# Projection of a transformer layer: weight loads, their low parts, rope sums and low parts of N on other engines

## The chip, the cores and the metric

The kernel runs on one core of one Trainium2 chip. The metric is the time of one execution on the device, in microseconds (us). The engines are TensorE (PE in the profile), VectorE (DVE), ScalarE (ACT), GpSimd (POOL) and SyncE (SP), which issues transfers; each has a queue of its own, worked off in order, and they meet only at semaphores.

## The reference

A macaron layer on x of 2048 tokens by 512: half a mixture of experts, attention, half a mixture of experts.

```python
x = x + 0.5 * _L0_ffn_ref(_layernorm(x), router_w, w1, w2, w3)      # 8 experts, top 2
x = x + _L0_attn_ref(_layernorm(x), wq, wk, wv, wo)
x = x + 0.5 * _L0_ffn_ref(_layernorm(x), router_w, w1, w2, w3)

# in _L0_attn_ref: 16 heads of 32 for q, 4 for k and v, causal
q = (x @ wq).reshape(b, t, QH, HD).transpose(0, 2, 1, 3)
k = (x @ wk).reshape(b, t, KVH, HD).transpose(0, 2, 1, 3)
v = (x @ wv).reshape(b, t, KVH, HD).transpose(0, 2, 1, 3)
q = apply_rope(q, cos, sin)      # x * c + rotate_half(x) * s
k = apply_rope(k, cos, sin)
```

All is fp32. The stage that this change touches is the layer norm before attention, the products with wq, wk, wv, and the rope.

## The kernel before

The program has stages, one after the other on every engine: a first norm and router, the experts (39 blocks of 128 rows, whose results are scattered to a tensor `y` in device memory, two halves of 2048 rows), the projection, attention, a second router, the experts again. The projection is written in `sp_project`, `pool_project`, `dve_project`, `act_project` and `pe_project`.

**Tiles.** The projection works on 16 tiles of 128 tokens. For tile i the input is three parts, x rows and the two halves of y, summed into `p.X[:, i % 4]` (four buffers, `XA` in the trace). For tiles 0 to 3, SP loads the halves into `ST` and VectorE adds them (L1150). For tiles 4 to 15, SP loads the x rows and GpSimd issues two adding transfers of y, one after the other (L1132): the first waits for the x rows, the second for the first.

**Precision.** A fp32 matrix product is made for tiles 1 to 13 from three passes of fp32r operands: high part times high part, high times low, low times high. `WQ` is the weights in fp32, `WH` (`WQH`) their high part, a cast by ScalarE, and `WL` (`WQL`) the difference WQ - WH. Tiles 0, 14 and 15 use one fp32 pass on `WQ`. The rotated q and k are stacked in `N` (`NA`): ScalarE writes the rounded high part twice (L1249, L1251, semaphore `ndup`) and the difference, the low part, is written beside it (L1196, L1197, semaphore `pN`).

**One turn i** of each engine, in the order of its queue:
- VectorE: row maxima of tops (`dve_top`, L965 and L967), found maxima, `norm(i+2)` (statistics), then `rope_split(i)`: two products of rope (L1182 to L1184, semaphore `rope`), their sum `t1 += t2` (L1186, `rsum`), `low(i+1)` (L1171), `scale(i+2)` (L1165), the low parts of N (L1196, L1197). `rope_split(i)` begins by waiting for `pN` of tile i-1, since `t1` is used again.
- ScalarE: the turned tile as high part, the square root for tile i+2, five copies of the stacked tile i-1 to `Qs` and `Ks` (L1239), V (L1244), the high parts of N, and, where maxima are found, `mT` (L1004).
- TensorE: projection i, transposes of tile i+1, stack of tile i-1 (20 transposes, L1330). Between the products of projections from tile 5 on it computes 6 tops (L952), scores of attention's first groups of which VectorE takes the maxima; they share three PSUM banks with the stack.
- SP: x rows of tile i, the rope table of tile i (`turns(i)`, waits for rope(i-3)), and the found maxima of tile i-3 (`sp_found`): a store of `mT` to device memory, a wait for it, a load into `Qs`. So the x rows of tile i+4 are issued behind rope(i), and behind `sp_found` where tile i has one. Maxima are found in turns 7, 10, 12 and 15.
- GpSimd: for tile i+4 the two adding transfers; four memsets of `Ks` rows (L1135), one behind each of rows 6 to 9.

**The start.** All engines wait until the last scatters of the experts have landed (`all_written`). SP then issues the rows of tile 0, the three weight loads, and the rows of tiles 1 to 3. ScalarE casts the weights after root(0), turned(0) and root(1); GpSimd computes `WL`.

**Memory.** `WQ` lies at the start of the area `A_T`, `XA` behind it; the area is shared with buffers of the experts.

Of the kernel before, what the change touches and what calls it, by code (L numbers as in the profile page):

```python
# [11 lines left out]
NJ = 39  # L12
# [197 lines left out]
def memory(nc, ctx, g):  # L210
    ctx.enter_context(nc.sbuf_tensor("fence", [P, (END - BASE) // 4 - 8], F32))
    keep = Area(nc, KEEP, END)
    g.Kc = keep("K", [P, C_PAD + 2])
    g.KB = keep("KB", [P, CBW], BF16)
    g.RT = keep("RT", [P, 4 * HD])
    g.PM = keep("PM", [P, 2, 16, 4])
    g.NM = keep("NM", [P, 16])
    g.M2 = keep("M2", [P, 4, 2, 4], F32R)
    g.mT = nc.alloc_sbuf_tensor_at("mT", [8, BQ], F32R, offset=keep.at)
    g.SM = keep("SM", [P, BQ])  # L220
    g.ones = keep("ones", [P, HD])
    g.ident = g.Kc[:, C_ID:C_ID + P]

    low = Area(nc, Q0, Q2)
    g.X = low("X0", [P, NT, D])
    g.R0 = router_memory(0, low, Area(nc, E_BIG, KEEP), 2)
    g.W = [weight_memory(nc, 0, Q0, Q2, A_K), weight_memory(nc, 1, Q3, Q1, Q0)]
    g.r = [route_memory(nc, f) for f in range(2)]
    g.x = [expert_memory(nc, f) for f in range(2)]

    g.Qs = [nc.alloc_sbuf_tensor_at(f"Qs{b}", [P, QH, BQ], F32R, offset=Q0 + 32 * KB1 * b) for b in range(NB)]
    g.Ks = nc.alloc_sbuf_tensor_at("Ks", [P, KVH, T], F32R, offset=A_K)
    g.V = nc.alloc_sbuf_tensor_at("V", [P, NT, P], F32, offset=A_V)
# [848 lines left out]

def sp_project(g):
    s, sp, d, p = g.s, g.nc.sync, g.d, g.p
    all_written(g, sp.wait_ge)

    x = d["L0_attn_x"].rearrange("b t d -> (b t) d")

    def rows(i):
        if i >= 4:  # L1090
            sp.wait_ge(s("paT"), i - 3)
        sp.dma_start(p.X[:, i % 4, :], x[i * P:i * P + P, :]).then_inc(s(f"xa{i % 4}"), 16)
        if i < 4:
            for h in range(2):
                sp.dma_start(p.ST[:, 2 * i + h, :], g.yd[T * h + i * P:T * h + i * P + P, :]).then_inc(s(f"st{i}"), 16)

    def turns(i):
        if i >= 3:
            sp.wait_ge(s("rope"), i - 2)
        sp.dma_start(p.cs[:, i % 3, :], d["rope"][i * P:i * P + P, :]).then_inc(s(f"cs{i % 3}"), 16)  # L1100

    rows(0)
    for name, o, n in (("wq", 0, 512), ("wk", 512, 128), ("wv", 640, 128)):
        sp.dma_start(p.WQ[:, :, o:o + n], d[f"L0_attn_{name}"].rearrange("(k p) n -> p k n", p=P)).then_inc(s("wqkv"), 16)
    turns(0)
    for i in range(1, 4):
        rows(i)
    for i in range(1, NT + 4):
        if 4 <= i < NT:
            rows(i)  # L1110
        if i < NT:
            turns(i)
        for G in g.found.get(i - 3, ()):
            sp_found(g, G)


def pool_project(g):
    s, pool, p = g.s, g.nc.gpsimd, g.p
    all_written(g, pool.wait_ge)

    pool.memset(g.ones[:], 1.0).then_inc(s("ones"), 1)
    for j, (o, n) in enumerate(((0, 512), (512, 256))):
        pool.wait_ge(s("wqh"), j + 1)
        pool.tensor_tensor(p.WL[:, :, o:o + n], p.WQ[:, :, o:o + n], p.WH[:, :, o:o + n].bitcast(F32),
                           ALU.subtract).then_inc(s("wql"), 1)
    for i in range(4, NT):
        b = i % 4
        pool.wait_ge(s(f"xa{b}"), 16 * (i // 4 + 1))
        for h in range(2):
            if h:  # L1130
                pool.wait_ge(*halves_on(g, i, 1))
            pool.dma_start(p.X[:, b, :], g.yd[T * h + i * P:T * h + i * P + P, :], accum_op=ALU.add).then_inc(  # L1132
                halves_on(g, i, h + 1)[0], 16)
        if 6 <= i < 6 + KVH:
            pool.memset(g.Ks[96:98, i - 6, :].bitcast(F32), 1.0).then_inc(s("kone"), 1)  # L1135


def dve_project(g):
# [34 lines left out]
    def rope_split(i):  # L1173
# [8 lines left out]
        dve.tensor_tensor(hd(p.t1[:]), qk, p.cs[:, b, 0:32].unsqueeze(1).to_broadcast([P, 20, HD]), ALU.mult)  # L1182
        dve.tensor_tensor(hd(p.t2[:])[:, :, 0:16], qk[:, :, 16:32], turn(32), ALU.mult)
        dve.tensor_tensor(hd(p.t2[:])[:, :, 16:32], qk[:, :, 0:16], turn(48), ALU.mult).then_inc(s("rope"), 1)  # L1184
        dve.wait_ge(s("rope"), i + 1)
        dve.tensor_tensor(p.t1[:], p.t1[:], p.t2[:], ALU.add).then_inc(s("rsum"), 1)  # L1186
        if in_parts(i + 1):
            low(i + 1)
        r = hd(p.t1[:])
        if i + 2 < NT:  # L1190
            scale(i + 2)
        dve.wait_ge(s("rsum"), i + 1)
        dve.wait_ge(s("ndup"), i + 1)
        if i:
            dve.wait_ge(*turned_from_n(g, i - 1))
        dve.tensor_tensor(p.N[:, 0:16, 64:96], r[:, 0:16, :], Nf[:, 0:16, 0:32], ALU.subtract)  # L1196
        dve.tensor_tensor(p.N[:, 16:20, 32:64], r[:, 16:20, :], Nf[:, 16:20, 0:32], ALU.subtract).then_inc(s("pN"), 1)  # L1197

    norm(0)
    scale(0)  # L1200
    norm(1)
    scale(1)
    for i in range(NT + 1):
        for _, key in g.fill[i]:
            dve_top(g, key)
        for G in g.found[i]:
            dve_found(g, G)
        if i + 2 < NT:
            norm(i + 2)
        if i < NT:  # L1210
            rope_split(i)


def act_project(g):
# [26 lines left out]
    def doubled(i):  # L1241
# [5 lines left out]
        if i:  # L1247
# [3 lines left out]
        act.copy(p.N[:, 16:20, :].rearrange("p h (a d) -> p h a d", d=HD)[:, :, 0:3:2, :],  # L1251
                 r[:, 16:20, :].unsqueeze(2).to_broadcast([P, 4, 2, HD])).then_inc(s("ndup"), 1)

    root(0)
    turned(0)
    root(1)
    act.wait_ge(s("wqkv"), 48)
    for o, n in ((0, 512), (512, 256)):
        act.copy(p.WH[:, :, o:o + n], p.WQ[:, :, o:o + n]).then_inc(s("wqh"), 1)
    for i in range(NT + 1):  # L1260
        if i + 1 < NT:
            turned(i + 1)
# [669 lines left out]
```

## Time and profile before

| | |
|---|---|
| runs | 1379.84, 1383.33, 1377.25 us |
| median | 1379.84 us |
| profiled execution | 1382.4 us, its span 1381.1 us |
| TensorE busy in the span | 1221.9 us, 88% |
| VectorE | 884.9 us, 64% |
| ScalarE | 661.7 us, 48% |
| GpSimd | 551.0 us, 40% |
| granted TensorE clock, mean | 0.958 of full speed |

The span is from the first to the last instruction of one execution. A busy share over the whole span is a mean over stages with different limits, so a stage is read by windows, by the timeline and by the chain of waits, each limited to it. Line numbers (L1184) are those of the kernel before. In the timeline a name such as `XA<-y` says what is written from what; in square brackets stand the idle time of the engine just before, and what ended it.

### The profile page before, as it was taken

How to read it: one execution, taken by the hardware profiler on the slowest of the kernel's cores; microseconds unless marked ns; L12 is line 12 of the kernel's file. 1: busy time of each engine (PE TensorE's matmuls, PEld its weight loads, DVE VectorE, ACT ScalarE, POOL GpSimd, SP SyncE). 2: the span in 40 equal slices, each digit the busy share in tenths (PEclk: the TensorE clock that was granted, in tenths of full speed). 3: DMA queues.
4: the chain of work that ended last, by engine and by line, in shares of the span. 5: the costliest groups of instructions: out<-in, count | busy, mean ns of one | idle time of the engine just before them, and what ended most of it. 6: DMA issues, size and time to landing. Idle time of an engine off the chain costs nothing.

```text
span 1381.1 us, 22056 instructions
## 1 busy us (share of the span) xinstructions
PE 1221.9 (88%) x7484; PEld 784.2 (57%) x7484; DVE 884.9 (64%) x2056; ACT 661.7 (48%) x1313; POOL 551.0 (40%) x458
## 2 busy tenths in 40 slices
PE   4499999679888999999989999999999849988884
PEld 4478888557775554454445455454433347766663
DVE  7867777479996665666676675667620375655662
ACT  2545555335455543454355454465567524444441
POOL 5635444223110110013344454527458653444443
PEclk8689999889999999999999999999999969999998
DMA  9723333355540021042013003023000343555554
GB/s 333 312 92 107 107 109 110 110 136 96 89 67 32 2 63 32 32 93 32 32 62 63 2 1 124 1 93 62 2 1 1 133 184 84 91 90 93 90 89 61
DMA packets 56891, 114.42 MB, mean 83 GB/s; under 512 B 7664, under 2 KB 17136, under 8 KB 56752
## 3 DMA queue, kind: packets, MB, share of 16 engines
q0 software_dynamic: 26112, 68.17, 22.5%
q1 hardware_dynamic: 30672, 44.85, 9.6%
q8 instruction: 64, 1.05, 0.3%
q14 instruction: 43, 0.35, 0.1%
HBM read 79.71 MB, written 33.55 MB: 82 GB/s over the span
## 4 chain that ended last, share of the span: by engine, by line
PE 57%; DMA 19%; DVE 14%; issue 5%; ACT 4%; SPq 1%; POOL 0%; POOLq 0%; DVEq 0%; ACTq 0%
DMA out<-Y,DI 13%; PE bank L1493 10%; PE bank L1505 10%; PE bank L797 8%; PE bank L952 8%; PE bank L1518 5%; PE bank L820 4%; PE bank L1555 3%; DVE PM L965 3%; DMA XA<-y 2%; DVE bank L967 2%; PE bank L779 1%; ACT P L1597 1%; PE bank L1535 1%; PE bank L1313 1%
## 5 line engine op out<-in xcount | busy, mean ns | idle before, releaser
L1597 ACT ACTIVATE P<-bank 128x512 f32<-128x512 f32 (+3 forms) x640 | 305.6, 536 | 299.6 <-PE bank L1493 295.5
L965 DVE TENSOR_REDUCE PM<-bank 128x1 f32<-128x512 f32 x384 | 252.8, 685 | 100.6 <-PE bank L952 99.6
L1493 PE MATMUL bank<-Qs,Ks 98*128 98x512 f32 (+3 forms) x640 | 248.5, 413 | 8.0 <-ACT P L1597 6.3
L952 PE MATMUL bank<-Ks,Qs 96*128 96x512 f32 (+3 forms) x640 | 238.9, 392 | 8.8 <-DVE PM L965 5.3
L1493 PEld LDWEIGHTS bank<-Qs,Ks 98*128 98x128 f32 x640 | 117.6, 190 | 151.3 <-issue 86.0
L1651 POOL TENSOR_TENSOR CH<-CH,P 128x512 f32<-128x512 f32 x128 | 160.3, 1286 | 71.9 <-ACT P L1597 71.0
L1636 POOL TENSOR_SCALAR_AFFINE_SELECT P<-P 128x512 f32<-128x512 f32 x64 | 40.9, 638 | 308.5 <-ACT P L1597 308.5
L967 DVE CUSTOM_DVE_ANT_0 bank<-bank,KB 128x128 f32<-128x128 f32 (+3 forms) x256 | 124.7, 497 | 57.8 <-PE bank L952 57.0
L952 PEld LDWEIGHTS bank<-Ks,Qs 96*128 96x128 f32 x640 | 121.9, 191 | 63.0 <-DVE PM L965 32.2
L1505 PE MATMUL bank<-P,V 128*32 128x512 f32 (+3 forms) x1280 | 152.5, 548 | 0.2 <-POOL P L1636 0.2
L908 DVE TENSOR_TENSOR DL<-W,DH 128x512 fp32r<-128x512 f32 x152 | 98.4, 689 | 46.4 <-ACT DH L869 33.7
L762 POOL DMA_INDIRECT out<-Y,DI x39 | 64.6, 1657 | 124.7 <-DMA out<-Y,DI 98.7
L735 POOL DMA_INDIRECT XG<-xn,TK x78 | 94.0, 1205 | 50.5 <-issue 21.9
L869 ACT CAST DH<-W 128x512 fp32r x152 | 86.8, 618 | 25.4 <-issue 25.4
L1518 PE MATMUL bank<-P,ones 128*32 128x512 f32 (+3 forms) x896 | 96.7, 503 | 0.0
L797 PE MATMUL bank<-WH,XH 128*128 x312 | 94.0, 423 | 3.0 <-ACT XH L849 2.0
L797 PE MATMUL bank<-WL,XH 128*128 x312 | 87.3, 402 | 0.1
L797 PE MATMUL bank<-WH,XL 128*128 x312 | 87.0, 401 | 0.0
L890 DVE TENSOR_TENSOR XL<-bank,XH 128x512 fp32r<-128x512 f32 x78 | 53.9, 691 | 46.3 <-ACT XH L849 46.3
L849 ACT CAST XH<-bank 128x512 fp32r<-128x512 f32 x78 | 45.8, 587 | 67.8 <-PE bank L779 64.9
L759 POOL DMA_INDIRECT y<-Y,DI x39 | 38.3, 983 | 98.2 <-DVE Y L916 98.2
L779 PE MATMUL bank<-K,XG 128*128 128x128 f32 x312 | 49.4, 282 | 28.6 <-DMA XG<-xn,TK 28.6
(184 smaller groups left out, 1903.3 us busy)
## 6 DMA issues: line engine op xcount, KB each, us to landing
xn<-XN SPq DMA_DIRECT2D x8, 1024.0 KB, 6.7
WR<-L_ffn_w POOLq DMA_DIRECT2D x16, 512.0 KB, 15.5
XO<-y POOLq DMA_DIRECT2D x8, 1024.0 KB, 9.6
WR<-L_ffn_w SPq DMA_DIRECT2D x16, 512.0 KB, 7.6
XA<-y POOLq DMA_DIRECT2D x24, 256.0 KB, 4.2
W<-L_ffn_w POOLq DMA_DIRECT2D x8, 512.0 KB, 25.0
XA<-L_attn_x SPq DMA_DIRECT2D x16, 256.0 KB, 3.4
XO<-L_attn_x SPq DMA_DIRECT2D x4, 1024.0 KB, 7.9
```

What stands on the lines that cost most here:

```text
L735: pool.indirect_dma_start(out=x.XG[:, j % NG, :], out_offset=None, in_=g.xnd[f][:, :], in_offset=bass.IndirectOffsetOnAxis(ap=r.TK[:, j:j ...
L797: ins = pe.matmul(bk(g, 2 + j % 2), part[:, k * P:k * P + P], w[:, bass.ds(ev[j] * 2048 + k * 512, 512)], start=(n == 0 and k == 0), stop= ...
L869: act.copy(x.DH[:, k, :], W.W3[:, bass.ds(e * 1024 + k * 512, 512)]).then_inc(s("dh"), 1)
L908: ins = dve.tensor_tensor(x.DL[:, k, :], W.W3[:, bass.ds(e * 1024 + k * 512, 512)], DHf[:, k, :], ALU.subtract)
L952: pe.matmul(bk(g, bank)[:, 0:n], g.Qs[b][0:96, G % 4 * 4 + h, c * P:c * P + P], g.Ks[0:96, G % 4, k * BQ:k * BQ + n], start=True, stop=Tru ...
L965: dve.tensor_reduce(dst, bk(g, bank)[:, 0:n], AX.X, ALU.max).then_inc(s(f"free{bank}"), 1)
L967: dve.tensor_tensor_reduce(out=bk(g, bank)[:, 0:n], in0=bk(g, bank)[:, 0:n], in1=g.KB[:, CB_MASK + BQ - n:CB_MASK + BQ], scale=1.0, scalar ...
L1493: pe.matmul(bk(g, i % 3)[:, o:BQ], g.Ks[0:98, G % 4, k * P:k * P + P], g.Qs[G // 4][0:98, G % 4 * 4 + j, o:BQ], start=True, stop=True).the ...
L1505: ins = pe.matmul(bk(g, 3)[32 * h:32 * h + 32, o:BQ], g.V[:, k, q * HD:q * HD + HD], a.P4[buffer_of(n)][:, h, o:BQ], start=(k == 0), stop= ...
L1518: ins = pe.matmul(bk(g, 4)[32 * h:32 * h + 32, o:BQ], g.ones[:], a.P4[buffer_of(n)][:, h, o:BQ], start=fresh, stop=last)
L1597: act.activation(a.P4[buffer_of(n)][:, j, o:BQ], bk(g, i % 3)[:, o:BQ], ACT.Exp, scale=scale).then_inc(s("exp"), 1)
L1651: ins = pool.tensor_tensor(to[:, h, :], two[:, h, :], one[:, h, :], ALU.add)
```

## The change

- SP issues the three loads of `WQ` at the head of `sp_project`, when TensorE's last expert product is done (`yp`), ahead of the wait for the scatters. For that `XA` and `WQ` change places in memory: `WQ` then overlaps only expert buffers that are read by then, and `XA` lies where GpSimd's scatter offsets were.
- ScalarE casts the weights first, before root(0).
- `WL` is computed by VectorE, after scale(1), instead of by GpSimd.
- The rope sum and the low parts of N go from VectorE to GpSimd. GpSimd's loop now runs over the turns i = 0 to 15: wait rope(i), sum; first adding transfer of tile i+4; memset where i is 6 to 9, and a wait for it; low parts of N; second adding transfer of tile i+4.

```diff
     t = Area(nc, A_T, KEEP)
+    p.X = t("XA", [P, 4, D])
     p.WQ = t("WQ", [P, 4, 768])
-    p.X = t("XA", [P, 4, D])
...
 def sp_project(g):
+    sp.wait_ge(s("yp"), NJ)
+    for name, o, n in (("wq", 0, 512), ("wk", 512, 128), ("wv", 640, 128)):
+        sp.dma_start(p.WQ[:, :, o:o + n], d[f"L0_attn_{name}"].rearrange("(k p) n -> p k n", p=P)).then_inc(s("wqkv"), 16)
     all_written(g, sp.wait_ge)
...
     rows(0)
-    for name, o, n in (("wq", 0, 512), ("wk", 512, 128), ("wv", 640, 128)):
-        sp.dma_start(p.WQ[:, :, o:o + n], d[f"L0_attn_{name}"].rearrange("(k p) n -> p k n", p=P)).then_inc(s("wqkv"), 16)
     turns(0)
...
 def pool_project(g):
-    for j, (o, n) in enumerate(((0, 512), (512, 256))):
-        pool.wait_ge(s("wqh"), j + 1)
-        pool.tensor_tensor(p.WL[:, :, o:o + n], p.WQ[:, :, o:o + n], p.WH[:, :, o:o + n].bitcast(F32),
-                           ALU.subtract).then_inc(s("wql"), 1)
-    for i in range(4, NT):
-        b = i % 4
-        pool.wait_ge(s(f"xa{b}"), 16 * (i // 4 + 1))
-        for h in range(2):
-            if h:
-                pool.wait_ge(*halves_on(g, i, 1))
-            pool.dma_start(p.X[:, b, :], g.yd[T * h + i * P:T * h + i * P + P, :], accum_op=ALU.add).then_inc(
-                halves_on(g, i, h + 1)[0], 16)
+    def half_on(i, h):
+        if h:
+            pool.wait_ge(*halves_on(g, i, 1))
+        else:
+            pool.wait_ge(s(f"xa{i % 4}"), 16 * (i // 4 + 1))
+        pool.dma_start(p.X[:, i % 4, :], g.yd[T * h + i * P:T * h + i * P + P, :], accum_op=ALU.add).then_inc(
+            halves_on(g, i, h + 1)[0], 16)
+
+    for i in range(NT):
+        pool.wait_ge(s("rope"), i + 1)
+        pool.tensor_tensor(p.t1[:], p.t1[:], p.t2[:], ALU.add).then_inc(s("rsum"), 1)
+        if i + 4 < NT:
+            half_on(i + 4, 0)
+        pool.wait_ge(s("rsum"), i + 1)
         if 6 <= i < 6 + KVH:
             pool.memset(g.Ks[96:98, i - 6, :].bitcast(F32), 1.0).then_inc(s("kone"), 1)
+            pool.wait_ge(s("kone"), i - 5)
+        pool.wait_ge(s("ndup"), i + 1)
+        if i:
+            pool.wait_ge(*turned_from_n(g, i - 1))
+        pool.tensor_tensor(p.N[:, 0:16, 64:96], r[:, 0:16, :], Nf[:, 0:16, 0:32], ALU.subtract)
+        pool.tensor_tensor(p.N[:, 16:20, 32:64], r[:, 16:20, :], Nf[:, 16:20, 0:32], ALU.subtract).then_inc(s("pN"), 1)
+        if i + 4 < NT:
+            half_on(i + 4, 1)
...
 def dve_project(g):
-        dve.wait_ge(s("rope"), i + 1)
-        dve.tensor_tensor(p.t1[:], p.t1[:], p.t2[:], ALU.add).then_inc(s("rsum"), 1)
         if in_parts(i + 1):
             low(i + 1)
-        r = hd(p.t1[:])
         if i + 2 < NT:
             scale(i + 2)
-        dve.wait_ge(s("rsum"), i + 1)
-        dve.wait_ge(s("ndup"), i + 1)
-        if i:
-            dve.wait_ge(*turned_from_n(g, i - 1))
-        dve.tensor_tensor(p.N[:, 0:16, 64:96], r[:, 0:16, :], Nf[:, 0:16, 0:32], ALU.subtract)
-        dve.tensor_tensor(p.N[:, 16:20, 32:64], r[:, 16:20, :], Nf[:, 16:20, 0:32], ALU.subtract).then_inc(s("pN"), 1)
+
+    def weights():
+        for j, (o, n) in enumerate(((0, 512), (512, 256))):
+            dve.wait_ge(s("wqh"), j + 1)
+            dve.tensor_tensor(p.WL[:, :, o:o + n], p.WQ[:, :, o:o + n], p.WH[:, :, o:o + n].bitcast(F32),
+                              ALU.subtract).then_inc(s("wql"), 1)
...
     scale(1)
+    weights()
...
 def act_project(g):
+    act.wait_ge(s("wqkv"), 48)
+    for o, n in ((0, 512), (512, 256)):
+        act.copy(p.WH[:, :, o:o + n], p.WQ[:, :, o:o + n]).then_inc(s("wqh"), 1)
     root(0)
     turned(0)
     root(1)
-    act.wait_ge(s("wqkv"), 48)
-    for o, n in ((0, 512), (512, 256)):
-        act.copy(p.WH[:, :, o:o + n], p.WQ[:, :, o:o + n]).then_inc(s("wqh"), 1)
```

## Rows read from the trace of the kernel before

**Rows 1.** The windows between turns: from:to, length, busy time of each engine, clock, DMA

```profile
265.59:295.35 29.76, 10.81 (x33) 6.54 (x34) 16.39 (x29) 4.52 (x7) 8.51 (x4) 0.71 0.52 180
295.35:325.93 30.58, 27.99 (x183) 24.36 (x183) 26.29 (x62) 17.56 (x39) 7.96 (x8) 0.95 0.55 100
325.93:353.75 27.82, 24.86 (x164) 21.00 (x163) 27.02 (x85) 13.82 (x32) 9.58 (x9) 1.00 0.53 89
353.75:373.23 19.48, 16.89 (x114) 14.42 (x113) 17.71 (x54) 9.66 (x23) 3.51 (x5) 1.00 0.54 87
383.07:403.44 20.37, 16.91 (x114) 14.43 (x113) 18.35 (x58) 9.66 (x23) 3.95 (x5) 1.00 0.46 83
403.44:429.62 26.18, 25.68 (x147) 19.56 (x145) 22.39 (x67) 13.57 (x30) 0.34 (x1) 1.00 0.10 14
```

**Rows 2.** The chain that ended last, start of the stage: start us, us, what

```profile
287.74 4.94 DVE XA L1150
```

**Rows 3.** Timeline (start us, us, engine, line, operation) and landing of one weight load

```profile
281.17 7.21 PE L1313 MATMUL bank<-WQ,SM 128*128 128x512 f32 x16 [0.68 <-ACT SM L1228]
287.45 7.43 POOL L1124 TENSOR_TENSOR WQL<-WQ,WQH 128x2048 fp32r<-128x2048 f32 x2 [17.84 <-ACT WQH L1259]
...
WQ<-L_attn_wv SPq DMA_DIRECT2D x1, 256.0 KB, 8.8
```

**Rows 4.** Timeline of VectorE in turns 4 and 7

```profile
328.25 1.11 DVE L1165 TENSOR_SCALAR XA<-XA,mvA,smA 128x512 f32<-128x512 f32 x1
...
352.13 0.83 DVE L1182 TENSOR_TENSOR t<-bank,cs 128x640 f32<-128x640 f32 x1
...
353.79 0.83 DVE L1186 TENSOR_TENSOR t<-t,t 128x640 f32<-128x640 f32 x1
...
356.53 0.68 DVE L1196 TENSOR_TENSOR NA<-t,NA 128x512 fp32r<-128x512 f32 x1
357.13 0.28 DVE L1197 TENSOR_TENSOR NA<-t,NA 128x128 fp32r<-128x128 f32 x1
```

**Rows 5.** Timeline of TensorE and VectorE, the tops; in brackets idle time and releaser

```profile
330.48 0.50 PE L952 MATMUL bank<-Ks,Qs 96*128 96x512 f32 x1 [0.55 <-DVE PM L967]
...
409.42 0.43 DVE L967 CUSTOM_DVE_ANT_0 bank<-bank,KB 128x256 f32<-128x256 f32 x1 [0.17 <-PE bank L952]
```

**Rows 6.** Timeline of GpSimd, first additions in turns 4, 6, 7, 9, 10

```profile
329.33 0.85 POOL L1132 DMA_DIRECT2D XA<-y  x1 [0.26 <-DMA XA<-L_attn_x]
...
349.44 0.85 POOL L1132 DMA_DIRECT2D XA<-y  x1 [3.00 <-DMA XA<-L_attn_x]
...
361.85 0.85 POOL L1132 DMA_DIRECT2D XA<-y  x1 [7.03 <-DMA XA<-L_attn_x]
...
379.24 0.85 POOL L1132 DMA_DIRECT2D XA<-y  x1 [5.25 <-issue]
...
391.85 0.85 POOL L1132 DMA_DIRECT2D XA<-y  x1 [7.31 <-DMA XA<-L_attn_x]
```

**Rows 7.** Timeline of SP's queue, the x rows of tile 11

```profile
358.95 0.36 SPq L1092 DMA_DIRECT2D XA<-L_attn_x  x1
```

**Rows 8.** Instructions of one line: count, duration ns min/median/max, first and last start

```profile
L553 POOL TENSOR_TENSOR WL<-WR,WH x4: 4523/4536/4562, 36.6 to 50.0; 128x2048 fp32r<-128x2048 f32 x4
L553 DVE TENSOR_TENSOR WL<-WR,WH x1: 2286/2286/2286, 59.9 to 59.9; 128x2048 fp32r<-128x2048 f32 x1
...
L1135 POOL MEMSET Ks<- x4: 1802/1806/1815, 319.9 to 344.6; 2x2048 f32 x4
...
L1651 POOL TENSOR_TENSOR CH<-CH,P x128: 1252/1278/1473, 650.2 to 1071.2; 128x512 f32<-128x512 f32 x128
```

**Rows 9.** Windows as in rows 1, about two gaps of TensorE

```profile
267.00:268.00 1.00, 0.00 (x0) 0.00 (x0) 0.00 (x0) 0.00 (x0) 0.60 (x1) 0.86 0.00 0
...
1258.00:1260.00 2.00, 2.00 (x8) 1.71 (x7) 0.54 (x1) 0.59 (x1) 0.22 (x1) 0.50 0.79 146
```

**Rows 10.** Timeline of VectorE, low parts of the last tile

```profile
432.00 0.69 DVE L1196 TENSOR_TENSOR NA<-t,NA 128x512 fp32r<-128x512 f32 x1 [1.51 <-ACT NA L1251]
```

More of the change, by code:

```diff
@@ L1121, in pool_project @@
     pool.memset(g.ones[:], 1.0).then_inc(s("ones"), 1)
-    for j, (o, n) in enumerate(((0, 512), (512, 256))):
-        pool.wait_ge(s("wqh"), j + 1)
-        pool.tensor_tensor(p.WL[:, :, o:o + n], p.WQ[:, :, o:o + n], p.WH[:, :, o:o + n].bitcast(F32),
-                           ALU.subtract).then_inc(s("wql"), 1)
-    for i in range(4, NT):
-        b = i % 4
-        pool.wait_ge(s(f"xa{b}"), 16 * (i // 4 + 1))
-        for h in range(2):
-            if h:
-                pool.wait_ge(*halves_on(g, i, 1))
-            pool.dma_start(p.X[:, b, :], g.yd[T * h + i * P:T * h + i * P + P, :], accum_op=ALU.add).then_inc(
-                halves_on(g, i, h + 1)[0], 16)
+    hd = lambda ap: ap.rearrange("p (h d) -> p h d", d=HD)
+    Nf = p.N[:].bitcast(F32)
+    r = hd(p.t1[:])
+    def half_on(i, h):
[11 more added lines that the diff above has]
+        pool.wait_ge(s("rsum"), i + 1)
         if 6 <= i < 6 + KVH:
             pool.memset(g.Ks[96:98, i - 6, :].bitcast(F32), 1.0).then_inc(s("kone"), 1)
+            pool.wait_ge(s("kone"), i - 5)
[6 more added lines that the diff above has]
+            half_on(i + 4, 1)
 def dve_project(g):
```

## The prediction

> **What bounds the kernel now.** The page puts 88% of the span on TensorE, but that is an average; the change touches one stage, so I read the windows whose borders are the rope turns of the projection [rows 1]. I call tile i's turn complete at R(i), the end of the second half of `t2` on VectorE (L1184), a little over 1.6 us after its beginning: R(0) = 295.35, R(4) = 325.93, R(7) = 353.75, R(9) = 373.23, R(10) = 383.07, R(12) = 403.44, R(15) = 429.62 us, and attention starts at 436.63. The windows show four regimes. Up to R(0) TensorE works 10.8 of 29.8 us: the stage waits for data. From R(0) to R(4), four turns in 30.58 us, VectorE has 4.3 us spare. From R(4) to R(7), three turns in 27.82 us, VectorE is busy 27.02 us: it is the bound, 9.3 us a turn. From R(12) on TensorE is (25.68 of 26.18 us). Outside 265.59 to 436.63 us nothing is changed.
>
> The chain of waits of the start [rows 2] runs through one addition on VectorE that takes 4.94 us; its twin just before took about 0.7. Beside it [rows 3] GpSimd computes the low weights from 287.45 to 294.88: the addition ends with GpSimd's first piece.
>
> **Part 1, the start.** New order: the three weight loads are issued at about 265.6, when TensorE's last expert matmul is done, instead of 270.8 to 272.3; ScalarE casts them first; VectorE makes the low parts after scale(1); GpSimd's 7.43 us there are gone. R(0) worked out: rows of tile 0 are issued as before, after the scatters have landed, so norm(0) starts at about 274.9 and scale(0) ends at 279.2 as before. Tile 1's halves no longer queue behind 1.5 MB of weights, so norm(1) and scale(1), 4.2 us together, run directly behind: end 283.5. Low weights on VectorE: 3072 elements at the rate of the 2048 in 2.29 us [rows 8], 3.4 us, end 286.9. norm(2), 2.5 us without the blocked addition, ends 289.4; TensorE's first projection ends at 288.4 [rows 3], so it isn't later. The rope multiplications take 1.62: R(0) = 291.1, a gain of 4.25 us. Bounds: the last weight load took 8.8 us to land [rows 3]; at that price the cast ends at 278.7 and sits in front of root(0), 1.2 us of the gain gone. Above, 5.5 us if tile 0 isn't delayed and VectorE is the only limit.
>
> The trace shows the blocking as whole waits, not a slowdown. By the Trainium skill (SBUF — State Buffer, Who interferes with whom) a VectorE instruction with two SBUF inputs contends with a GpSimd instruction that reads SBUF, and one of them blocks for a whole instruction; the 4.94 us addition agrees. By that rule the same lock returns with each rope sum on GpSimd, against `scale`; that is a rival below.
>
> **Part 2, what leaves VectorE in each turn.** The rope sum (0.83 us busy) and the two low parts of N (0.68 and 0.28) [rows 4]; by the starts of what followed them they are 0.74 + 0.80 = 1.54 us a turn. The rope multiplications before them take 1.62, from 352.13 to R(7). This is worth 1.54 us only if nothing is right behind. TensorE is: between R(4) and R(5) it waited for VectorE only 0.55 us, and between R(12) and R(13) VectorE already waited for TensorE's sixth and last top [rows 5], which it took at R(12)+6.0; with 0.35 for it, 1.05 for the statistics and 1.62 for the rope that turn lasted 9.0 us, VectorE idle in it. The sixth top is 256 or 512 columns wide in turn, so TensorE's loop gives 8.8 to 9.2. VectorE's 9.3 can fall to that, 0.1 to 0.5 us a turn, not by 1.5.
>
> **Part 3, the order on GpSimd.** This is the step on which I stake the forecast. GpSimd's queue for turn i is now: wait rope(i), sum; wait for the landing of x rows i+4, issue the first addition of y; memset (i = 6 to 9); wait `ndup`, low parts of N; wait for the first addition to land, issue the second. VectorE's rope(i+1) waits `pN` from the low parts. So the low parts, which need only R and the copies of ScalarE, stand behind the landing of x rows, which SP issues only after rope(i) and, in turns 7 and 10, after the round trip of the maxima. Terms:
> - GpSimd's rates [rows 8]: 2048 elements 4.54 us, 512 elements 1.28 us, so 2.12 ns an element and 0.19 fixed. Sum of 640: 1.55. Low parts 512 + 128: 1.28 + 0.46 = 1.74. An issue 0.85, the memset 1.81, both seen.
> - When the first issue for tile i+4 came, after R(i) [rows 6]: 3.4 (turn 4), 4.9 (turn 6), 8.1 (turn 7), 6.0 (turn 9), 8.8 (turn 10). In turn 7 the round trip holds back the x rows to 358.95, R+5.2 [rows 7]; it begins after ScalarE's copies, which now follow GpSimd's slower sum, +0.65.
> - Turn length by this loop = that moment + 0.9 issue + (1.9 memset) + 1.74 + 0.1 + 1.62 rope = moment + 4.4, or + 6.3 with memset.
>
> Turn by turn against before: turns 0 to 3 have moments of 3.4 to 4.0, so 7.8 to 8.4 against 7.5 to 7.9: +1.8 in all. Turns 4 and 5 are held by TensorE's loop: -0.2. Turns 6, 8 and 9: the longer turns leave the transfers more room, so I take 4.4 between the seen 3.4 and 6.0: 10.7 each against 9.24, 10.04 and 9.84, +3.0. Turn 7: 8.1 + 0.65 + 6.3 = 15.05 against 9.44, +5.6. Turn 10: 8.8 + 0.65 + 4.4 = 13.8 against 8.99, +4.8. Turn 11 before was 11.4 because x was late, and now x is early: about 10.5, -0.9. Turns 12 to 14 issue nothing for a later tile and TensorE bounds them: 0. Tail: between R(15) and attention the low parts are on the path, begun at 432.00 after ScalarE's copies [rows 10]; the sum (1.55 for 0.83, of which ScalarE hid some) and the low parts (1.74 for 0.8) give +1.8.
>
> TensorE now idles about 6 us in turn 7 and 4 in turn 10. After TensorE's last expert matmul at 265.6 its granted clock averaged 0.86 in the window 267 to 268, and a shorter gap near 1256 was followed by a window at 0.50, which is 1.2 GHz of 2.4, with TensorE busy in all of it [rows 9]. I estimate 1.7 us of work lost per such restart, from about 3.4 us at that level; it falls beside GpSimd's waiting in turn 8 and I have put it into turn 11's 10.5.
>
> Sum: -4.25 + 1.8 - 0.2 + 3.0 + 5.6 + 4.8 - 0.9 + 1.8 = +11.65, say +12 us. The profiled execution has a span of 1381.1 us in 1382.4; it becomes about 1393 in 1394.5. The median of the runs shown is 1379.84, so I forecast 1392.
>
> Unknown costs, from both sides. The low parts of N are written in pieces of 32 elements, which no GpSimd row shows: not under the 1.74 us of contiguous rows; above, I take up to 2.6 (half as much again), 0.9 us in some nine turns, +8. The moments of turns 6, 8, 9 at 3.4: -3; as seen (4.9, 5.2, 6.0): +2.9. The clock: 0 to +3. The start: -1.2 to +1.2. Together 1384 to 1402 for this case.
>
> **The rivals.**
> - A, faster: x rows are landed early enough and the stage stays VectorE's. From the turn's budget (rope to rope 9.3, rope itself 1.6) the low parts may end as late as R+5.9 to 7 without cost; with a moment of 3.4 they end at R+6.0. For it: turns 0 and 4 with moments of 3.4. Against it: the two round trips, which no spare VectorE time shortens, and TensorE's loop. If the full 1.54 us came in turns 4 to 11: -4.25 - 12.3 + 1.8 = -14.8, 1365 us. It decides if pN comes before R+6.1 in nearly every turn. 12 in 100 for anything below 1373.
> - B, a wash: the start gives 4.25, only the two round trips cost, and their delay is partly given back since VectorE catches up: -4.25 - 1 + 7 + 1.8 = +3.5, 1383 us. For it: turn 11's slack. 20 in 100.
> - C, GpSimd's pieces of 32 cost double, 3.5 us: +1.75 in ten turns above the forecast, 1409 us. Nothing in the trace speaks for it but the absence of a row. 7 in 100.
> - D, the lock of part 1 comes back: `scale` (which took 1.11 us in turn 4 beside GpSimd's memset [rows 4]) waits for each rope sum. GpSimd may start a sum 1 us late, behind its issue, so scale ends up to 1.1 us later, and the tops with it; where VectorE has no slack that is 8 x 1.1 = +9 over the forecast, 1401 us. The skill's rule above is the same mechanism. 6 in 100.
> - E, the start gains nothing, as the early weights only delay tile 0's rows: forecast + 4.25, 1396 us; 5 in 100.
>
> **How the numbers follow.** The forecast has 50 in 100. A measurement of this kernel can tell about 0.5%, 6.9 us, from no change. Slower by more (above 1386.7): the forecast, C, D and E, 68 in 100. Within: B, 20. Faster: A, 12. The range reaches from just under B to the upper bounds: 1380 to 1402.
>
> **What would show it.** Right: the low weights gone from GpSimd, R(0) near 291; in turns 7 and 10 rope(i+1) starts 13 and 12 us after R(i), waiting for GpSimd's low parts, behind an issue that waited for XA; memset between issue and low parts in turns 6 to 9; TensorE idle for `NA` there, with half clock after. Wrong: rope(i+1) nowhere waits for pN, or turns 4 to 9 are near 8 us (A); the low parts last 2.5 us or more (C); scale stretched in every turn with VectorE full (D).

## The result, and the profile after

The changed kernel took 1400.88 us (median of 4 runs, 1398.0 to 1405.95) against 1379.8 (median of 4 runs, 1377.25 to 1383.33): ratio 1.0155, 95% interval 1.0117 to 1.0193. (The ratio is that of the means.) It is slower, as forecast, by 21 us where 12 were forecast. The profiled execution took 1398.0 us, its span 1396.8, granted clock 0.958 on average, as before.

The page of the changed kernel, its span and busy times:

```profile
span 1396.8 us, 22056 instructions
PE 1223.9 (88%) x7484; PEld 787.0 (56%) x7484; DVE 865.9 (62%) x2010; ACT 665.2 (48%) x1313; POOL 596.6 (43%) x504
```

VectorE lost 19 us of work and GpSimd gained 46; TensorE's share did not move. The page says who works, not who waits, so the reading is again by windows. These answer to [rows 1]: the start, turns 0 to 3, then turns 6, 7, 8, 9 and 10 one by one (turn i goes from R(i) to R(i+1); in the changed kernel R(i) is the end of L1199), turns 12 to 14, and the tail from R(15) to attention. The columns are from:to, length, busy time of TensorE, of its weight loads, of VectorE, ScalarE and GpSimd, granted clock, busy share of the DMA engines and GB/s.

```profile
263.60:293.06 29.46, 10.46 (x26) 5.74 (x27) 15.46 (x32) 4.52 (x7) 1.08 (x2) 0.65 0.55 182
293.06:326.10 33.04, 27.25 (x187) 23.80 (x185) 22.24 (x52) 17.83 (x38) 19.37 (x19) 1.00 0.53 93
344.10:354.47 10.37, 7.99 (x54) 7.05 (x53) 8.81 (x29) 4.84 (x11) 7.67 (x7) 0.97 0.47 83
354.47:369.78 15.31, 10.18 (x55) 8.76 (x54) 7.83 (x25) 5.03 (x11) 6.72 (x6) 0.83 0.31 55
369.78:381.89 12.11, 9.31 (x61) 8.41 (x60) 7.35 (x26) 5.41 (x12) 6.69 (x6) 0.92 0.41 71
381.89:393.89 12.00, 10.37 (x62) 8.95 (x61) 8.79 (x28) 5.33 (x13) 6.66 (x6) 0.89 0.48 72
393.89:406.98 13.09, 8.13 (x49) 7.00 (x48) 7.34 (x25) 4.42 (x10) 4.10 (x4) 0.93 0.31 61
418.49:444.73 26.24, 25.75 (x147) 19.61 (x145) 18.34 (x59) 13.95 (x30) 9.69 (x9) 1.00 0.04 8
444.73:454.58 9.85, 4.62 (x27) 3.88 (x25) 0.00 (x1) 7.18 (x13) 3.20 (x3) 0.83 0.02 5
```

Turn 7 shows the new state: in 15.31 us TensorE works 10.2, VectorE 7.8, ScalarE 5.0, GpSimd 6.7. No engine is the bound; they wait for each other. In turns 12 to 14, where nothing is fetched for a later tile, the time is that of before (26.24 against 26.18). Turn 7 on the timeline, GpSimd, SP, TensorE and VectorE in order of time:

```profile
354.55 1.53 POOL L1137 TENSOR_TENSOR t<-t,t 128x640 f32<-128x640 f32 x1 [0.99 <-DVE t L1199]
...
360.56 0.36 SPq L1095 DMA_DIRECT2D XA<-L_attn_x  x1
...
363.58 0.85 POOL L1132 DMA_DIRECT2D XA<-y  x1 [7.49 <-DMA XA<-L_attn_x]
364.48 1.80 POOL L1142 MEMSET Ks<- 2x2048 f32 x1
366.36 1.26 POOL L1147 TENSOR_TENSOR NA<-t,NA 128x512 fp32r<-128x512 f32 x1
367.58 0.45 POOL L1148 TENSOR_TENSOR NA<-t,NA 128x128 fp32r<-128x128 f32 x1
...
368.09 3.76 PE L1343 MATMUL bank<-K,NA 128*96 128x128 f32 x20 [5.13 <-POOL NA L1148]
368.17 0.82 DVE L1197 TENSOR_TENSOR t<-bank,cs 128x640 f32<-128x640 f32 x1 [3.90 <-POOL NA L1148]
```

GpSimd's sum is done 1.6 us after R(7). Then the queue stands for 7.49 us at the wait for the x rows, which SP issued at 360.56; issue, memset and low parts follow one after the other, and both TensorE's stack and VectorE's next rope start when the second low part ends, 368.0. The waits of the stage from 293 to 455 us (who waited for what: total us, times, longest):

```profile
POOL XA L1132 <- DMA XA<-L_attn_x: 29.5, 9, 7.5
...
PE bank L1343 <- POOL NA L1148: 28.4, 12, 5.1
...
DVE t L1197 <- POOL NA L1148: 14.0, 9, 4.0
```

Where the time went, in the two profiled executions (before, after; us):

| part of the stage | before | after | difference | forecast |
|---|---|---|---|---|
| last expert product of TensorE to R(0) | 29.77 | 29.46 | -0.3 | -4.25 |
| turns 0 to 3 | 30.58 | 33.04 | +2.5 | +1.8 |
| turns 4, 5 | 18.58 | 18.00 | -0.6 | -0.2 |
| turns 6, 8, 9 | 29.12 | 34.48 | +5.4 | +3.0 |
| turn 7 | 9.44 | 15.31 | +5.9 | +5.6 |
| turn 10 | 8.99 | 13.09 | +4.1 | +4.8 |
| turn 11 | 11.38 | 11.51 | +0.1 | -0.9 |
| turns 12 to 14 | 26.18 | 26.24 | +0.1 | 0 |
| R(15) to attention | 7.01 | 9.85 | +2.8 | +1.8 |
| sum | 171.05 | 190.98 | +19.9 | +11.65 |

The spans differ by 15.7: outside the stage this one execution of after was 4.2 us shorter (2.0 before it, 2.2 behind it). The experiments show such differences in both directions, so I read the stage against itself and leave them.

### The profile page after: what moved, and what is told of

Read it like the earlier page. It is cut to its first block, busy times and chain, and to the rows that moved or that the text cites. A ratio compares the mean times of both kernels' runs of the same rounds, so it can differ in the third digit from the quotient of the medians.

```text
span 1396.8 us, 22056 instructions
## 1 busy us (share of the span) xinstructions
PE 1223.9 (88%) x7484; PEld 787.0 (56%) x7484; DVE 865.9 (62%) x2010; ACT 665.2 (48%) x1313; POOL 596.6 (43%) x504
## 4 chain that ended last, share of the span: by engine, by line
PE 63%; DMA 14%; DVE 12%; issue 5%; POOL 3%; ACT 3%; SPq 0%; POOLq 0%; DVEq 0%; ACTq 0%
PE bank L797 10%; PE bank L1506 10%; PE bank L1518 9%; DMA out<-Y,DI 9%; PE bank L952 8%; PE bank L1531 5%; PE bank L820 5%; PE bank L1568 3%; DVE PM L965 3%; PE bank L1326 2%; PE bank L779 2%; DMA XA<-y 1%; PE bank L1343 1%; ACT P L1610 1%; DVE bank L967 1%
## 5 line engine op out<-in xcount | busy, mean ns | idle before, releaser
L1343 PE MATMUL bank<-K,NA 128*96 128x128 f32 x320 | 46.2, 306 | 30.6 <-POOL NA L1148 28.4
## 6 DMA issues: line engine op xcount, KB each, us to landing
WR<-L_ffn_w POOLq DMA_DIRECT2D x16, 512.0 KB, 15.7
```

## The experiments

Two kinds of number follow. The stage's parts come from one profiled execution of each kernel; the medians and ratios from several runs beside the kernel before on the same chip. The medians of before there were 1380.15 us (e1 to e4), 1381.05 (e5 to e8) and 1378.87 (e9 to e11). The ratios are those on record for each kernel; they aren't the quotients of these medians (for e2 and e3 the quotients are higher, 1.012 and 1.016). The tail ends with TensorE's first attention matmul.

| kernel | median us | ratio (95%) | start to R(0) | R(0) to R(15) | tail |
|---|---|---|---|---|---|
| before | 1379.8 | | 29.77 | 134.27 | 7.01 |
| after | 1400.88 | 1.0155 (1.0117 to 1.0193) | 29.46 | 151.67 | 9.85 |
| e1 start only | 1377.91 | 0.9973 (0.9949 to 0.9998) | 29.49 | 135.13 | 7.00 |
| e2 turns only | 1396.86 | 1.0091 (1.0060 to 1.0123) | 28.43 | 154.52 | 9.67 |
| e3 low parts ahead | 1401.71 | 1.0120 (1.0077 to 1.0164) | 29.41 | 155.52 | 10.34 |
| e4 memsets early | 1394.79 | 1.0092 (1.0066 to 1.0117) | 28.63 | 145.84 | 9.93 |
| e5 after, no additions | 1374.42 | 0.9959 (0.9936 to 0.9982) | 29.13 | 126.60 | 9.43 |
| e6 before, no additions | 1376.25 | 0.9950 (0.9919 to 0.9981) | 29.75 | 128.90 | 7.02 |
| e7 start in order | 1374.74 | 0.9965 (0.9944 to 0.9986) | 25.20 | 132.71 | 8.06 |
| e8 low parts shared | 1371.27 | 0.9919 (0.9887 to 0.9951) | 24.77 | 129.80 | 7.76 |
| e9 after, x rows first | 1387.90 | 1.0072 (1.0049 to 1.0096) | 29.14 | 142.93 | 10.49 |
| e10 after, sums back | 1402.07 | 1.0172 (1.0133 to 1.0212) | 29.34 | 151.73 | 9.64 |
| e11 e7, x rows first | 1370.36 | 0.9944 (0.9925 to 0.9964) | 26.36 | 132.47 | 8.41 |

**Each part alone.** My theory: the start gains, and GpSimd's order costs in the turns. Rival: the start gains nothing (E). e1 takes the first half of the change (memory, loads, casts, low weights on VectorE), e2 the second.

```diff
  e1: before, and
+ sp: the three loads of WQ behind yp, ahead of all_written
+ act: casts of WQ ahead of root(0);   dve: WL in weights() behind scale(1)
- pool: WL
  e2: before, and pool_project and the end of each turn of dve_project as in the change
```

> The start of the change alone (weight loads at the end of the experts, casts first, low weights by VectorE after scale(1)); rope sums and low parts of N stay on VectorE, GpSimd issues only the additions and memsets. Theory 'the loads delay the scatters': in the changed kernel the last scatters landed 7.6 us after their issue where they took 2.7 before, so the rows of tile 0 start 5 us late and the gain of the start is spent: from TensorE's last expert matmul to R(0) 29.5 us against 29.77 before, stage and time unchanged within 1 us. Rival, my prediction's part 1: R(0) 4.25 us earlier, time about 1375.5 us (-0.3%).

> The other half alone: loads, casts and low weights as before, rope sums and low parts of N on GpSimd in the order of the change. Theory 'all of the loss is in the turns': R(0) to R(15) 151 to 152 us against 134.3 before, tail 9.8 against 7.0, the whole stage +20 us, time +1.4 to +1.5%. Rival 'start and turns make each other worse' (rows of tiles 0 to 3 come differently): less than +15 us here.

e1: start 29.49 us, so the early loads gave nothing. The ratio of 0.9973 is 0.3% below before, which the stage (171.62 us against 171.05) doesn't account for. e2: turns 154.5 us, 20 more than before and 2.5 above what I expected, with turns 7 and 10 at 15.5 and 14.0; the ratio of 1.0091 lies under the 1.4 to 1.5% expected. The loss is in the turns and the tail, not in the start. Why the start fails is seen in when GpSimd goes on after the last scatters of the experts (issue, then the first instruction behind the landing). e1:

```profile
267.65 0.96 POOL L759 DMA_INDIRECT y<-Y,DI  x1 [1.53 <-DVE Y L916]
274.94 0.12 POOL L1122 MEMSET ones<- 128x32 f32 x1 [6.34 <-DMA y<-Y,DI]
```

The kernel before:

```profile
266.64 0.96 POOL L759 DMA_INDIRECT y<-Y,DI  x1 [1.52 <-DVE Y L916]
269.49 0.12 POOL L1121 MEMSET ones<- 128x32 f32 x1 [1.89 <-DMA y<-Y,DI]
```

The last scatter is waited for until 7.3 us after its issue where it was 2.9, with 1.5 MB of weights in the transfers beside it; every engine waits for it (`all_written`), and counted from TensorE's last expert product tile 0's rows start 4.4 us later. The thirteen traces divide without exception: the seven kernels with early loads wait 7.0 to 7.6 us, the six others 2.8 or 2.9.

**The start in another order.** If that is the cause, the weights must be kept behind the scatters and behind the rows of tiles 0 and 1, and VectorE's part of the gain must come back.

```diff
  e7: before, and
     rows(0)
+    rows(1)
     (loads of WQ as before; casts as before)
+ dve: WL in weights() behind scale(1);   - pool: WL
```

> The kernel before with the weight loads behind the rows of tiles 0 and 1 (and, as before, behind the scatters), casts where they were, and low weights by VectorE behind scale(1). Theory 'the early loads spent the gain by delaying the scatters': here the scatters land in 2.7 us and VectorE is not blocked by GpSimd, so from TensorE's last expert matmul to R(0) 25.6 us against 29.8; stage and time -4 us, ratio 0.997. Rival 'the start is bound by the bytes to load whatever their order': R(0) within 1 us of before.

GpSimd in e7, at the same place:

```profile
265.72 0.96 POOL L759 DMA_INDIRECT y<-Y,DI  x1 [1.52 <-DVE Y L916]
268.56 0.12 POOL L1122 MEMSET ones<- 128x32 f32 x1 [1.88 <-DMA y<-Y,DI]
```

The start is 25.20 us, 4.6 less than before, and the scatter lands as it did. The gain that I worked out for the start exists; the early loads were what took it away. Its size moves between traces: e8 and e11 have the same start and took 24.77 and 26.36 us. In e11 TensorE's first projection waited 2.30 us for the last weight load, in e7 0.94. e7 makes two edits at once, and no run parts them; nor does any run move the loads alone, without the casts and the low weights.

**The low parts ahead of the addition.** If the low parts suffer only from standing behind the x rows, putting them first should win most of the loss.

```diff
  e3: after, in pool_project
-        if i + 4 < NT:
-            half_on(i + 4, 0)
...
         pool.tensor_tensor(p.N[:, 16:20, 32:64], ...).then_inc(s("pN"), 1)
+        if i + 4 < NT:
+            half_on(i + 4, 0)
         (memset behind this, then half_on(i + 4, 1))
```

> The changed kernel with the low parts of N ahead of the first addition and of the memset in GpSimd's queue; the same work on the same engines. Theory 'order': the low parts end at about R+5.0 in every turn, turns 7 and 10 fall from 15.3 and 13.1 to 9 or 10 us, the clock stays high there; the first addition moves back from R+3.4 to 4.9 to at least R+5.0, which makes the early turns 8.3. Stage +5 us over before instead of +20, time +0.3 to +0.4% against before. Rival 'place': the cost is GpSimd's slower sum and low parts and the restarts of the clock, not the order; then at least +14 us remain.

I was wrong: 155.5 us in the turns, no better than after, and the stage 24 us over before, which the rival 'place' had asked for (at least +14); e5 and e6 below decide between the two. GpSimd in turn 5 of e3, and the sum of turn 6:

```profile
346.07 1.27 POOL L1142 TENSOR_TENSOR NA<-t,NA 128x512 fp32r<-128x512 f32 x1 [1.52 <-issue]
347.29 0.46 POOL L1143 TENSOR_TENSOR NA<-t,NA 128x128 fp32r<-128x128 f32 x1
347.69 0.84 POOL L1132 DMA_DIRECT2D XA<-y  x1
352.26 0.86 POOL L1132 DMA_DIRECT2D XA<-y  x1 [3.73 <-DMA XA<-y]
352.85 1.88 POOL L1137 TENSOR_TENSOR t<-t,t 128x640 f32<-128x640 f32 x1
```

The low parts now start 1.5 us after the sum, but the wait for the first addition's landing, 3.73 us and formerly hidden in part under memset and low parts, now stands in front of the next rope sum, which starts 3.4 us after R(6) = 349.50. Sum 1.9, copies of ScalarE 1.5, low parts 1.7, first addition issued and waited for 4.6: about 10 us a turn, above the 9.3 of before (turns 1 to 6 took 9.7 to 10.2). The queue has two waits for transfers in each turn; moving the work round them changes which work pays.

The long turns hardly shrank either: turn 7 took 14.59 us and turn 10 13.56, where I had expected 9 or 10. In turn 7 the low parts were done at R(7)+8.6, but the next rope started only at R(7)+13.0, and not for want of them. ScalarE and TensorE in turn 7 of e3:

```profile
365.08 1.04 ACT L1263 CAST NA<-t 128x1024 fp32r<-128x1024 f32 x1 [3.74 <-POOL t L1137]
...
366.34 0.57 ACT L1004 CAST mT<-bank 8x512 fp32r<-8x512 f32 x1
...
366.96 0.33 PE L952 MATMUL bank<-Ks,Qs 96*128 96x128 f32 x1 [2.92 <-ACT mT L1004]
```

ScalarE's queue holds the copy `mT` behind the high parts of N, and these wait 3.74 us for GpSimd's late sum. TensorE's next top waits 2.92 us for `mT`, the remaining tops and VectorE's maxima follow, and the x rows of tile 11 are issued at R(7)+9.0. So a late sum on GpSimd has a second way to reach VectorE, through ScalarE and TensorE, in the turns in which maxima are found.

**The waits taken away.** e5 and e6 leave out the two additions of y for tiles 4 to 15, so for these tiles y isn't added; the work on the engines is otherwise the same.

```diff
  e5: after, and e6: before, with
-            half_on(i + 4, 0) / (i + 4, 1)        (e6: the dma_start of both halves)
...
-            dve.wait_ge(*halves_on(g, i, 2))
+            dve.wait_ge(s(f"xa{b}"), 16 * (i // 4 + 1))
```

> The changed kernel without the adding transfers of y for tiles 4 to 15 (those tiles are projected from the x rows alone, a part of the residual sum is left out): GpSimd's queue then holds only sums, memsets and low parts, the same work on the same engines, with no wait for a landing among it. Theory 'GpSimd is one serial queue, and waits for landings stand in it between work that VectorE's next turn awaits': turns 7 and 10 fall to 9.5 or less, the clock stays high, turns 4 to 11 are 8.9 to 9.2 each as TensorE allows; R(0) to R(15) 128 to 131 us instead of 151.7. Rival 'place': GpSimd's slower sum and low parts cost by themselves, R(0) to R(15) stays above 140.

> The kernel before with the same adding transfers left out, as the measure for the run above. VectorE holds turns 4 to 11 at 9.3 (no late rows: turns 8 and 11 lose their 0.7 and 2.0 us), turns 0 to 3 shrink to about 6.5 to 7; R(0) to R(15) about 128. Against it the changed kernel without additions should be between -3 and +3 us over R(0) to R(15) by the theory, and +12 or more by the rival.

GpSimd in turn 7 of e5, from R(7) = 348.90 on:

```profile
348.98 1.56 POOL L1137 TENSOR_TENSOR t<-t,t 128x640 f32<-128x640 f32 x1 [3.52 <-DVE t L1195]
350.60 2.05 POOL L1140 MEMSET Ks<- 2x2048 f32 x1
352.73 1.29 POOL L1145 TENSOR_TENSOR NA<-t,NA 128x512 fp32r<-128x512 f32 x1
```

With no landing to wait for, the moved work costs nothing: 126.6 us in the turns against 128.9 with the work on VectorE. With the landings the same move costs 17.4 (151.67 against 134.27). So 17 us of loss and 2 us of gain are told apart: the additions in GpSimd's queue are the loss, and the rival 'place' falls for the turns. e5 takes away their issues (0.85 us each) together with their waits; of the two, e4 and e9 below show what shorter or earlier waits give back, and no run takes away the issues alone. Only the tail stays longer, by 2.4 (9.43 against 7.02): the low parts of the last tile end 1.5 us later on GpSimd, whatever the transfers do, and the stack behind them took 3.59 us for 2.56, the clock again (last section).

**Which waits.** e4 moves the four memsets of GpSimd ahead of the loop, e9 lets SP issue the x rows of a tile ahead of the round trip of the found maxima, e10 gives the rope sums back to VectorE.

```diff
  e4: after
+    for h in range(KVH): ... pool.memset(g.Ks[96:98, h, :], 1.0)      ahead of the loop
-        if 6 <= i < 6 + KVH: memset, wait
  e9: after, in sp_project, turn i
-        if 4 <= i < NT:
-            rows(i)
         (found maxima)
+        (above them, behind the rope table)  if 4 <= i + 1 < NT: rows(i + 1)
  e10: after
-        pool: wait rope(i), sum        +  dve: wait rope(i), sum, as before
```

> The changed kernel with the four memsets ahead of GpSimd's loop (it idles there from the last scatter to rope(0)); nothing else moved. Theory 'order': turns 6 to 9 lose the 1.9 us that each memset with its wait puts ahead of the low parts: turn 6 9.1 (held by TensorE), 7 13.4, 8 and 9 10 to 10.5; stage about 7 us shorter than the changed kernel's, +13 over before. Rival 'the memsets lie beside the wait for the first addition': below 2 us of difference to the changed kernel.

> The changed kernel with SP issuing the x rows of tile i+4 ahead of the round trip of the maxima of tile i; nothing on GpSimd is changed. If the low parts of N stand behind the landing of x rows, the two long turns shrink by the 6 us that the round trip held the rows back: turn 7 from 15.3 to 10.5 to 11 (the memset stays), turn 10 from 13.1 to 9 or 9.3; turns 8 and 9 stay at 11 to 12; R(0) to R(15) 142 to 144 us instead of 151.7. Rival 'turns 7 and 10 are long because the maxima's own instructions and the half clock are there': they stay above 13.

> The changed kernel with the rope sums back on VectorE; the low parts of N stay on GpSimd behind the first addition. Theory 'the wait for x rows ahead of the low parts makes the loss, the sums little': turn 7 14.6, turn 10 12.4, turns 0 to 3 about 8.2, R(0) to R(15) 147 to 149 us, the tail 1 us shorter. Rival 'the sums on GpSimd make the serial queue too long': below 142 us.

e4: 145.84 us in the turns, 5.8 less than after, 2.8 of it in turn 7, 1.9 and 1.6 in turns 8 and 9: the memset was in the chain. e9: turn 7 fell from 15.31 to 10.41, turn 10 from 13.09 to 9.05, the turns together from 151.67 to 142.93. GpSimd in turn 7 of e9, whose R(7) is 358.01:

```profile
358.10 1.54 POOL L1137 TENSOR_TENSOR t<-t,t 128x640 f32<-128x640 f32 x1 [0.95 <-DVE t L1199]
362.21 0.86 POOL L1132 DMA_DIRECT2D XA<-y  x1 [2.57 <-DMA XA<-L_attn_x]
```

The wait at the same instruction is 2.57 us where it was 7.49, the issue at R(7)+4.2 and not +9.1. e10: 151.73 us, turns 7 and 10 at 15.0 and 13.1; I had expected 147 to 149. In the two long turns the sums play next to no part: while GpSimd stands at a landing, it doesn't matter whether it had a sum to do before. Elsewhere the equal total hides two changes: turns 8, 9 and 11 fell by 0.6, 1.1 and 1.2 us, and turns 1 and 2 rose by 2.9 in sum, where the first addition waited for its x rows until R+5.6 and R+5.5, not R+4.2 and R+4.0. e9 has the same in turn 1 (10.04 us); why they landed later was not tried. The issue in turn 7 of e10 waited longer, by the sum's 1.53 us and most of the 0.99 us idle before it:

```profile
366.95 0.86 POOL L1133 DMA_DIRECT2D XA<-y  x1 [9.75 <-DMA XA<-L_attn_x]
```

**A better version.** e8 keeps what the experiments leave standing: the start of e7, the x rows ahead of the round trip, the memsets ahead of the loop, the sums on VectorE, and only the low parts of turns 4 to 11 on GpSimd, where they stand ahead of the wait for the x rows of a tile and leave the two additions to overlap with the next turn. e11 is e7 with nothing but the x rows ahead.

```diff
  e8, pool_project
     for i in range(4, NT):
+        j = i - 4
+        if j in range(4, 12): wait rsum(j), ndup(j), stack(j-1); the low parts of N of tile j
         pool.wait_ge(s(f"xa{b}"), 16 * (i // 4 + 1)); first addition; wait; second addition
```

> The run above, and in addition: SP issues the x rows of tile i+4 ahead of the round trip of the maxima of tile i; memsets ahead of GpSimd's loop; low parts of N on GpSimd in turns 4 to 11 only, ahead of the first addition; rope sums stay on VectorE. By the theory of the serial queue nothing that VectorE awaits stands behind a landing for long: low parts end at R+4.3, turns 4 to 11 8.9 to 9.1 instead of 9.3 to 11.4, in all -5 us there, -4 at the start: stage 162 us instead of 171, time -0.6 to -0.7%. Rival 'any low part on GpSimd collides with the additions': turns 4 to 11 longer than before's 77.5 us in sum.

> The kernel before with the ordered start (weight loads behind the rows of tiles 0 and 1, low weights on VectorE) and x rows ahead of the round trip, GpSimd as before: what of the gain of the version with shared low parts is not GpSimd's. Start 25 us, turns 8 and 11 lose the rest of their wait, 9.4 each; R(0) to R(15) 131.5 to 132 us against 129.8 with shared low parts and 132.7 without the new order of SP; ratio 0.994 to 0.996.

e8 took 1371.27 us, ratio 0.9919 (0.9887 to 0.9951): 0.8% faster than before, where the change has a ratio of 1.0155. Its stage took 162.3 us, as expected, against 171.05. Turns 4 to 11 took 72.2 us against 77.5 before, and VectorE's rope waited for GpSimd's low parts in none of them. e11 took 1370.36, ratio 0.9944 (0.9925 to 0.9964), with 132.5 us in the turns and 75.3 in turns 4 to 11. In one execution each e8 is shorter by 2.7 us in the turns, 1.6 at the start and 0.6 in the tail; only the turns have to do with GpSimd. The intervals of the ratios overlap, so which of the two is faster isn't settled.

## Why the prediction was right, and where it was not

**The start: the step that failed.** The sentence "rows of tile 0 are issued as before, after the scatters have landed, so norm(0) starts at about 274.9" took the landing of the scatters as given. The chain of waits of after, at the start of the stage and in turn 7:

```profile
264.66 7.49 DMA y<-Y,DI
...
273.10 3.57 DMA ST<-y
...
360.56 2.74 DMA XA<-L_attn_x
...
364.48 1.81 POOL Ks L1142
...
366.36 1.26 POOL NA L1147
```

SP issues the three weight loads from 263.63 to 265.16; the scatter issued among them, at 264.66, is on the path for 7.49 us. The first addition of norm(0) starts 13.2 us after TensorE's last expert product, where the prediction had 9.3 (274.9 less 265.6): 3.9 us, all of the missing gain but 0.1. I had let SP's loads pass the scatters in SP's queue and had asked only what they do to tile 1's rows, not what they do to transfers already under way on GpSimd's side. This is rival E, to which I gave 5 in 100: right in its result (-0.3 us for -4.25), its wording too narrow, as the weights delayed the scatters rather than tile 0's rows. The other terms were sized well: from the start of norm(0) to R(0) the changed kernel took 16.3 us where the prediction had 16.2, and e7 gained 4.6 us.

**The order on GpSimd: right.** The rule "turn = moment of the first issue + 4.4, or + 6.3 with the memset" holds where nothing else was last: turn 6, 4.1 + 6.3 = 10.4 (measured 10.37); turn 7, 9.1 + 6.3 = 15.4 (15.31); turn 8, 5.9 + 6.3 = 12.2 (12.11); turn 10, 8.8 + 4.4 = 13.2 (13.09). Every step named for turn 7 is in the timeline above. For turn 9 the rule gives 11.2 where 12.00 was measured: its rope started 1.0 us after the low parts and waited for nothing. TensorE ran the first 2.7 us of this turn at half clock and its tops came late. e9, also at half clock there, took 11.96; e10, at full clock in turn 9, took 10.89, with a moment of 4.7 and the rule's 11.0.

**Mis-sized terms.** The moment taken for turns 6, 8 and 9 was 4.4; 4.1, 5.9 and 4.9 came, and with the 0.8 us of turn 9 this made +5.4 us in place of +3.0. "The longer turns leave the transfers more room" was a hope: the x rows of turn 8 are issued right behind rope(8), however long turn 7 was, and took 5 us to land:

```profile
370.21 0.43 SPq L1095 DMA_DIRECT2D XA<-L_attn_x  x1
...
375.68 0.85 POOL L1132 DMA_DIRECT2D XA<-y  x1 [4.28 <-DMA XA<-L_attn_x]
```

The bound from the moments as seen (+5.9) would have been closer. Turn 10 came out 0.7 less, since its moment stayed at 8.8 (I had added 0.65 for the slower sum). Turn 11 gave nothing back: its x was no longer late, but the stack of tile 10 at its head ran at half clock; e9, at full clock there, took 9.80. The prediction had put 1.7 us of clock into this turn and let nothing of it reach turn 9 or the tail. The tail cost 2.8, not 1.8: the low parts ended 1.5 us later, and the stack of the last tile ran at half clock, 3.97 us for the 2.57 of before:

```profile
449.59 3.97 PE L1343 MATMUL bank<-K,NA 128*96 128x128 f32 x20 [4.20 <-POOL NA L1148]
```

**What was luck.** 1400.88 is 1.1 us inside the upper end of the range, 1402. The stage came out 8.3 us over the sum, 3.9 of them at the start, where the bounds allowed 1.2. The range held because 8 of its upper microseconds stood there for slow pieces of 32 elements, which cost nothing. The order on GpSimd was foreseen; that the range held was in part luck.

**Part 2: right.** Taking 1.54 us a turn from VectorE was worth little: turns 4 and 5, which GpSimd didn't hold or held by 0.17 us, gained 0.6 us in two, inside the 0.1 to 0.5 a turn of the prediction. e5 against e6, 2.3 us over fifteen turns, says the same of all the turns.

**The rivals.** A (faster) fell: VectorE's rope waited for GpSimd's low parts nine times. B fell with the start and with turns 6, 8 and 9, which cost 5.4 us. C fell: the pieces of 32 elements took 1.26 and 0.45 us undisturbed, as the contiguous rows of [rows 8] had it (1.28 and 0.46). D was there, but in the wrong place: `scale` took 1.3 to 1.6 us in turns 1 to 4, 6 and 11, where the addition's issue held a sum back beside it, and 0.55 in turns 7 to 10. One of either kind:

```profile
302.43 1.43 DVE L1180 TENSOR_SCALAR XA<-XA,mvA,smA 128x512 f32<-128x512 f32 x1
...
355.92 0.55 DVE L1180 TENSOR_SCALAR XA<-XA,mvA,smA 128x512 f32<-128x512 f32 x1
```

In e5, without issues, it took 0.55 in each of those turns. In e10, with the issues but the sum on VectorE, it did too. `scale` reads one tensor and two columns of scalars, so the rule on two inputs that the prediction named isn't the one for it. By the Trainium skill (SBUF — State Buffer, Who interferes with whom), an instruction of its kind, `tensor_scalar`, can use the port pair that VectorE shares with GpSimd, and one side then blocks; the stretched rows agree. It had no price that I can separate: the turns in which it shows follow the loop's rule without it (turn 3: issue at R+4.0, + 4.4 = 8.4, measured 8.31), and where the large losses are it is absent.

## What to carry to other kernels

A queue that holds waits for transfers is a bad place for work that another engine waits for: here such work cost 17 us behind the landings and nothing without them, on an engine that is 43% busy on the page. Before moving work, list what the target's queue waits for in each turn and when that comes; then either the transfer's trigger moves earlier, or only such pieces go over as stand behind no landing. And a load that is issued earlier shares the transfers with whatever is then landing; if all engines wait for that landing, the load belongs behind it.

## What the runs showed of the hardware that was not expected

**Scatters beside large loads.** The last scatter of the experts was waited for until 2.9 us after its issue without loads beside it, and until 7.3 (e1) and 7.6 (after) where 1.5 MB of loads had been issued in the 1.1 us ahead of it. What in the transfers delays it (their order, or the memory) was not tried.

**The clock after short waits.** TensorE's granted clock fell after a wait of 5.13 us in turn 7, as the two windows show, and was back at 1.00 at 371. (Columns as in rows 1.)

```profile
367.00:368.00 1.00, 0.00 (x0) 0.00 (x0) 0.00 (x0) 0.00 (x0) 1.00 (x2) 0.76 0.16 25
368.00:369.00 1.00, 0.91 (x5) 0.88 (x6) 0.83 (x2) 0.00 (x0) 0.89 (x2) 0.50 0.00 0
```

It fell too after a wait of 2.79 us at the end of turn 8 (0.59 in 381 to 382, then 0.50, with TensorE busy in all of both). In the tail it depends on something that I did not find. The stack of the last tile waits 2.67 us for the low parts both before and in e8; its rows, and the windows behind them, before first:

```profile
432.95 2.57 PE L1330 MATMUL bank<-K,NA 128*96 128x128 f32 x20 [2.67 <-DVE NA L1197]
433.00:435.00 2.00, 2.00 (x17) 1.73 (x18) 0.00 (x0) 1.99 (x5) 0.00 (x0) 1.00 0.07 16
```

and e8:

```profile
422.91 3.46 PE L1350 MATMUL bank<-K,NA 128*96 128x128 f32 x20 [2.67 <-DVE NA L1210]
424.00:426.00 2.00, 2.00 (x12) 1.77 (x10) 0.00 (x0) 1.73 (x4) 0.00 (x0) 0.51 0.03 8
```

The same wait, once with full and once with half clock after it. The other traces divide too: after this wait of 2.67 us the stack took 2.56 or 2.57 us in before, e1 and e6, and 3.46 to 4.05 in e7, e8 and e11. The longer stacks account for the longer tails of e7, e8 and e11 against before (by 1.1, 0.8 and 1.4 us); whether they come with each execution, one profile of each can't say, and it stays open.
